# Three embedding blocks instead of six in the attention stage of a vision transformer, and one score tile ahead of the values

## What is computed

```
h = patches(x) @ W.T + b                  # 196 patches of 768 values -> 256, in f32
h = concat([cls_tok, h], axis=1)          # 197 tokens
h = h + attention(layernorm(h))           # 16 heads of 16 values, causal softmax
h = h + ffn(layernorm(h))                 # 3 cycles of a coupling network, f32
```

## Time and profile before

| what | value |
|---|---|
| median of 3 runs | 3649.94 us (3648.4 to 3652.1) |
| the profiled execution | 3651.66 us |
| its span, first to last instruction | 3649.9 us |
| granted TensorE clock over the span | 0.989 |
| busy share TensorE, VectorE, ScalarE, GpSimd | 97%, 85%, 66%, 50% |
| a step of the attention stage | about 19 us |

### The profile page before, as it was taken

One profiled execution on the slowest core, in us unless ns is written; L12 is line 12 of the kernel. 1 busy time (PEld: TensorE's weight loads), 2 busy tenths in 40 slices (PEclk: granted clock), 3 DMA queues, 4 the chain that ended last, 5 costly groups with the idle time before them and its releaser, 6 DMA issues.

```text
span 3649.9 us, 88155 instructions
## 1 busy us (share of the span) xinstructions
PE 3549.6 (97%) x30735; PEld 2676.6 (73%) x30990; DVE 3088.9 (85%) x7415; ACT 2422.8 (66%) x5698; POOL 1827.4 (50%) x2967
## 2 busy tenths in 40 slices
PE   7999999999999999999999999987999999999998
PEld 6888888888888888888888888875555555555554
DVE  6888888888888888888888888876989989989987
ACT  4777777777777777777777777774554555554554
POOL 5776677666776667766777667763001001001000
PEclk9999999999999999999999999988999999999999
DMA  3444444444444444444444444433222222212211
GB/s 102 119 120 106 117 115 120 114 111 116 117 120 112 114 113 120 116 111 114 117 120 115 113 117 115 120 88 81 65 65 78 71 58 81 75 55 80 73 45 54
DMA packets 298324, 361.76 MB, mean 99 GB/s; under 512 B 28192, under 2 KB 264992, under 8 KB 297888
## 3 DMA queue, kind: packets, MB, share of 16 engines
q1 hardware_dynamic: 297888, 356.11, 37.2%
HBM read 131.80 MB, written 53.26 MB: 51 GB/s over the span
## 4 chain that ended last, share of the span: by engine, by line
PE 86%; DVE 7%; DMA 2%; issue 2%; SPq 1%; ACT 0%; POOL 0%; DVEq 0%; another core or an unknown queue 0%; POOLq 0%
PE ps L1077 14%; PE ps L1411 11%; PE ps L1165 8%; PE ps L1126 7%; PE ps L1113 7%; PE ps L1420 6%; PE ps L1196 5%; PE ps L1150 5%; PE ps L1215 4%; PE ps L1205 3%; PE ps L1173 3%; PE ps L1435 2%; PE ps L1427 2%; PE ps L1154 2%; PE ps L1198 2%
## 5 line engine op out<-in xcount | busy, mean ns | idle before, releaser
L1077 PE MATMUL ps<-xb,w_tok 128*128 128x196 f32 x3072 | 686.3, 348 | 7.5 <-DMA clsT<-in_clsT 7.3
L1411 PE MATMUL ps<-X,cn_w 128*128 128x394 f32 x1536 | 584.9, 510 | 7.7 <-DVE X L1015 7.7
L886 DVE TENSOR_REDUCE mx<-ps 69x2 f32<-69x396 f32 x1024 | 518.0, 553 | 14.2 <-PE ps L1205 1.3
L592 ACT ACTIVATE p<-ps 128x394 f32<-128x394 f32 x1024 | 454.8, 499 | 74.6 <-PE ps L1126 65.3
L1077 PEld LDWEIGHTS ps<-xb,w_tok 128*128 128x128 f32 x3072 | 491.7, 192 | 8.0 <-DMA clsT<-in_clsT 7.3
L880 DVE TENSOR_REDUCE mx<-ps 128x4 f32<-128x512 f32 x512 | 337.6, 680 | 181.1 <-remote 180.2
L543 POOL TENSOR_SCALAR ve<-mv 128x4 f32<-128x4 f32 x64 | 20.2, 316 | 911.7 <-DVE mv L898 911.7
L1411 PEld LDWEIGHTS ps<-X,cn_w 128*128 128x128 f32 x1536 | 273.6, 189 | 258.0 <-issue 94.9
L537 POOL TENSOR_TENSOR h<-h,att 128x256 f32<-128x256 f32 (+1 forms) x256 | 186.9, 751 | 431.9 <-DVE att L875 431.9
L1126 PE MATMUL ps<-qZ,kT 128*128 128x396 f32 (+1 forms) x2048 | 382.5, 320 | 12.9 <-DMA qZ<-mx_scratch 11.0
L610 ACT ACTIVATE sq<-ps 128x256 f32<-128x256 f32 (+1 forms) x512 | 196.2, 383 | 247.1 <-PE ps L1113 247.1
(11 more groups left out here) (139 smaller groups left out, 8076.5 us busy)
## 6 DMA issues: line engine op xcount, KB each, us to landing
qZ<-qT SPq DMA_DIRECT2D x256, 396.0 KB, 5.2
xb<-in_x SPq DMA_DIRECT2D x128, 588.0 KB, 7.2
kZ<-kT SPq DMA_DIRECT2D x512, 128.0 KB, 2.6
h_scratch<-h SPq DMA_DIRECT2D x128, 128.0 KB
hl<-h_scratch SPq DMA_DIRECT2D x64, 256.0 KB
hk<-h_scratch SPq DMA_DIRECT2D x64, 256.0 KB
out<-hk SPq DMA_DIRECT2D x64, 256.0 KB
h_scratch<-h SPq DMA_DIRECT2D x128, 69.0 KB
```

The source lines that it names most:

```text
L592: s.activation(p0[:, i, 2 * jj:2 * jj + 2, :], ps[:, (b0, b1)[jj], 0:2 * TE].rearrange("p (a b) -> p a b", b=TE)[:, :, 0:T], ACT.Exp).then ...
L886: v.tensor_reduce(mx[:T1, 1, 4 * i + c:4 * i + 4:2], ps[:T1, SBANK[3 * i + 1 + c], 0:2 * TE].rearrange("p (a b) -> p a b", b=TE), AX.X, AL ...
L1077: mm = t_.matmul(ps[:, W[ft], 0:NP], w_tok[:, k, ft * P:ft * P + P], xb[:, par, k, :], start=k == 0, stop=k == KT - 1)
L1411: mm = t_.matmul(ps[:, 2 * c + mt, 0:N2], cn_w1[:, f, mt * P:mt * P + P], X[:, c, state(cyc), f, :], start=f == 0, stop=f == FT - 1)
```

## The change

It moves three embedding parts, so that parts (0, 0) and (0, 1), (0, 2) and (1, 0), (1, 1) and (1, 2) stand next to each other, with their waits. It moves `scores_first(m, 2)` from behind the values' products to ahead of them, with the wait for the padded k that it needs. And it exchanges banks 0 and 1 in several places: the first tile of group 2 goes to bank 1, whose maximum (the second) is taken earlier than that of bank 0 (the fourth), and the others that used these banks go to the other one. The number of instructions of each kind stays what it was, but for one wait.

```diff
-        SBANK = (6, 7, 0, 1, 2, 3, 0, 1, 2, 3, 0, 5)
-        MAX_OF = (4, 2, 5, 6, 7)
+        SBANK = (6, 7, 0, 1, 2, 3, 1, 0, 2, 3, 1, 5)
+        MAX_OF = (2, 4, 5, 6, 7)
         W = (6, 7)
-        KB, QB = (3, 4, 0, 5), (1, 2, 3, 4)
+        KB, QB = (3, 4, 1, 5), (0, 2, 3, 4)
         HB = (4, 5)
         PB = ((4, 6), (4, 7))
-        MB, CB = (7, 0), (1, 2)
+        MB, CB = (7, 1), (0, 2)
...
                 embed_part(0, 0)
+                embed_part(0, 1)
                 if there(m):
...
                     qk_transpose(k2, KB, 3)
                 elif there(n):
                     pe.wait_ge(qkv_ready, n * 4 + 4)
-                embed_part(0, 1)
...
                     qk_transpose(q2, QB, 0)
                     qk_transpose(q2, QB, 1)
                 embed_part(0, 2)
+                embed_part(1, 0)
                 if there(m):
                     pe.wait_ge(kT_ready, n * 4 - 3)
                     qk_transpose(q2, QB, 2)
                     pe.wait_ge(kT_ready, n * 4 - 2)
                     qk_transpose(q2, QB, 3)
 
-                embed_part(1, 0)
...
                     scoresT(o, r % 2, 0)
                 embed_part(1, 1)
+                embed_part(1, 2)
                 if there(o):
                     if there(m):
                         pe.wait_ge(qT_ready, n * 4)
                     scoresT(o, r % 2, 1)
-                embed_part(1, 2)
...
                     hn_transpose(x, 1)
+                if there(m):
+                    pe.wait_ge(kZ_loaded[1], n * 32)
+                    scores_first(m, 2)
                 if there(o):
...
                     pv(o, (r + 2) % 4, 1)
                 if there(m):
                     pe.wait_ge(kZ_loaded[1], n * 32)
-                    scores_first(m, 2)
                     scores_halves(m, 1 - r % 2, 2)
```

## The result

| | before | changed |
|---|---|---|
| median | 3649.89 us (4 runs, 3648.4 to 3652.1) | 3724.28 us (4 runs, 3723.1 to 3727.8) |
| ratio, with its 95% interval | | 1.0204 (1.0192 to 1.0217) |
| span of the profiled execution | 3649.9 us | 3723.3 us |
| granted TensorE clock over the span | 0.989 | 0.990 |

The changed kernel is 2.0% slower, 74 us. The prediction said 3753 with a range of 3690 to 3795.

A forecast was written before the change was run, and what follows sets the result against it. TensorE was taken to bound the kernel: 1.00 - 0.11 = 0.89 us a step over 123 steps, 109 us, minus 6 for late transfers, made 3754.7 profiled and a median of 3753 us (+2.8%). The range was 3690 to 3795.

The forecast's parts named there:

- What bounds it: TensorE in the attention stage, busy 493 of 500 us at clock 1.00; every wait put on it counts in full.
- The wait for h_ready: Embedding part (1,0), moved ahead, waits for VectorE's copies of h; first group of transposed scores 0.64 us late, or 0.41.
- Averaging the two kinds: TensorE's delay at the second score tile: 1.12 us in one sort of step, 0.89 in the other; taken as 1.00.
- ScalarE: Second scores group's exponentials start 1.30 us late (1.07 in the other sort of step); ScalarE idles 0.7 us before them.
- The 2.04 us between the two: From the second scores group's first exponential to the end of the third group's second; three exponentials take some 1.15 us.
- The wait that the prediction named: scores_first(m, 1), going into bank 1, waits for the third scores group's second exponential; TensorE 1.12 us late, or 0.89.
- The moved tile: First tile of group 2 ahead of the values: changed order of kinds of work, minus 0.11 us a step.
- main case: Slower, since the waits at embedding part (1,0) and the second score tile delay TensorE: 3729 to 3788 us, chance 0.75.
- the first rival: ScalarE catches up, so only the late first scores group counts: 0.41 us a step, 3700 us; chance 0.14.
- The clock: Rival: TensorE's granted clock falls because it now stands in every step; at 0.87, say, 4000 us; chance 0.02.
- Faster: Rival: h_ready costs nothing and gains of 0.03+0.11 us a step come in: 3633 us; chance 0.06.
- Joining blocks by itself: On TensorE, putting work of one kind together: minus 0.03 us a step (minus 0.10 to plus 0.01).

The follow-up runs named there:

- e3_tile_only: Changed kernel with all six embedding parts back in their old places; the moved score tile and exchanged banks stay. 3635.6 us, 0.9954 of the kernel before.
- e4_blocks_only: Changed kernel with the first tile of group 2 back behind the values, banks as changed. 3754.7 us, 1.0281 of the kernel before.
- e1_t10_back: Changed kernel with embedding part (1,0) back behind the second pair of q transposes. 3671.6 us, 1.0053 of the kernel before.
- e6_h_early: Changed kernel with VectorE's two copies of h ahead of the four small root mean square operations. 3666.8 us, 1.0050 of the kernel before.
- e5_first_block_tile: Changed kernel with parts (1,0) and (1,2) back: only parts (0,0) and (0,1) joined, tile moved. 3622.0 us, 0.9927 of the kernel before.
- e2_t12_back: Changed kernel with embedding part (1,2) back between the second and third groups of transposed scores. 3691.0 us, 1.0107 of the kernel before.

## Why the prediction was right, and where its sizes were off

- **What bounds it.** TensorE was busy without a gap, and each wait put on it came out in the time: right.
- **The wait for h_ready.** Right in place and kind. t10's load starts 0.06 us behind the copies; S0 ends at 1015.11 against 1007.36 + 7.33 = 1014.69, 0.42 late. The prediction had 0.41 for the second kind of step and 0.64 for the first, and took both as equally frequent. So they were before (the first kind, with the slow L838, in 54 of 121 steps), but the change made the second kind the commoner one (the first in 18 of 121; L838 has a mean of 304 ns after and 468 before). *Averaging the two kinds is the term of the sum that was sized wrong first*, by 0.11 us in the step shown, and by 0.08 over all.
- **ScalarE.** S1's exponentials start at 1016.69 against 1008.29 + 7.33 = 1015.62, 1.07 late, as worked out for this kind. The second exponential of S2 ends 0.92 late, not 1.02. *The 2.04 us between the two was the second wrong term*: with its input ready ScalarE starts a full-width exponential 0.28 us after the shorter one (1017.47 to 1017.75), where the prediction let three exponentials take 1.15. They take 1.06. Two more things the prediction did not see, and neither changed the sum. ScalarE does not stand 0.4 us in front of S0's exponentials, as it said, but not at all, for it still copies q; so it stands 0.54 and not 0.7 in front of S1's. And TensorE does not reach S3 unhindered: S3 waits for S1's own exponentials, and ends 0.61 late. The wait that the prediction named comes after that one and ends last. Two products of the second score tile end at 1019.18 against 1018.41: TensorE is 0.77 late, not 0.89.
- **The moved tile.** Of these 0.77 the step keeps 0.63. The prediction had minus 0.11, the rows say minus 0.14, and the steps of e3_tile_only and e4_blocks_only say 0.14 and 0.15. Right.
- **Sum.** 0.89 - 0.11 (kinds) - 0.10 (exponentials) - 0.03 (tile) = 0.65 against 0.63 read. These are why 3724 came out below the main case's own range, whose low end took the second kind everywhere and all of the tile's possible gain, but no faster exponentials; what holds it is the wider range, made for the first rival, which did not happen. Over 123 steps 0.63 makes 77 us, and the 18 steps of the longer kind add 4; the spans differ by 73. The rest fits fewer delayed steps: before, the mean of the steps was 0.09 above their median, and the wait for padded k, in it, went from 6.3 us to 0.7, where the prediction took off 6.
- **Rivals.** ScalarE did not catch up; e1_t10_back and e6_h_early each leave 0.2 us a step net of the tile's gain, from the late S1 alone. The clock stayed at 1.00. Faster was excluded by the copies of h, as said.
- **Joining blocks by itself.** 0.03 a step was forecast for the first block; e5_first_block_tile gives 0.06 in the step read, 0.03 between the medians of all steps, and 0.27% between the ratios, part of it late transfers. (The prediction's total of 0.03 for all blocks is a slip of 0.01: its terms are 0.03 and 0.01.) So a change of kind costs something here, 0.76 against 0.66 us for an embedding part. That it is the weight load that is not fully hidden was argued, and no run shows it. The Trainium skill (TensorE: Matmul & The Clock Gate, "Step-by-step: what each phase is for") says that weight loads are pulled ahead of matmuls in flight; if that were complete and nothing else differed, the 0.03 would be 0, and the steps say 0.03.

## What to carry to other kernels

A piece of work between two waits is also what hides them. Before moving it, list for each wait that it stands in front of when the data really came, not only whether the engine stood: here the trace showed no idle time at t10 and at the second score tile, and yet their weight loads started 0.12 and 0.08 us behind what they needed, where 0.06 and 0.05 is what a load that waits takes in the changed kernel. Where a second engine is fed in portions and its results are waited for, compare the distance from one portion to the next with what that engine takes for one: here filler between the first and the second portion starved it (1.70 us apart in the changed kernel, with 0.54 of ScalarE's time idle between), and the same filler one portion later cost nothing in the steps read. And undo a change part by part: the tile alone gave 0.5% and one block another 0.3% (part of it late transfers), while the whole lost 2.0%.

## What was not expected of the hardware

VectorE's two small operations L838 and L841 each have two durations, and their place decides whether GpSimd's addition L537 beside them is in the way. In the kernel before L838 takes 0.21 or 0.80 us and L841 0.23 or 0.57, for the same 128 x 64 elements. Durations in ns (min/median/max) of L841 in the changed kernel, and in the one with the copies of h early, where L841 comes after GpSimd's addition has ended:

```profile
L841 DVE TENSOR_TENSOR y<-y,xh x128: 225/571/578, 40.5 to 2521.8; 128x64 f32<-128x64 f32 x128
```

```profile
L841 DVE TENSOR_TENSOR y<-y,xh x128: 224/226/571, 41.7 to 2464.7; 128x64 f32<-128x64 f32 x128
```

In the first step of the earlier trace rows, GpSimd's two additions end at 1004.48 and L838, started at 1003.77, at 1004.57 (GpSimd's and VectorE's timelines of the kernel before):

```profile
1003.07 1.41 POOL L537 TENSOR_TENSOR h<-h,att 128x256 f32<-128x256 f32 x2 [3.21 <-DVE att L875]
```

```profile
1003.77 0.80 DVE L838 TENSOR_TENSOR y<-rs 128x64 f32<-128x64 f32 x1
```

The Trainium skill (SBUF — State Buffer, "SBUF: two separate sides") says that VectorE operations with two inputs in SBUF and GpSimd operations that read SBUF take a shared pair of ports as a lock for the whole instruction. The trace agrees: the slow operation ends 0.09 us behind GpSimd's, and in the next step, where L841 is the slow one, it is 0.09 again (1023.63 and 1023.54). Which of the two VectorE operations is caught changes the end of the copies by 0.25 us. The kernel before hid that (both kinds of step take 18.97); the kernels that wait on those copies show it as steps 0.24 us longer, the changed one in 18 of 121, e2_t12_back in 49 and e4_blocks_only in 47. What decides which is caught was not tried.
